# One sequence's attention steps moved five tiles forward in a one-core Macaron block

## The reference

```python
def ffn(x):                                   # 12 experts, 3 for each token
    topw, sel = jax.lax.top_k(x @ Wg, 3)
    cw = sum(softmax(topw) * one_hot(sel, 12))
    h = gelu(einsum('bsd,edh->ebsh', x, Wup) + bup)
    y = einsum('ebsh,ehd->ebsd', h, Wdown) + bdown
    return einsum('bse,ebsd->bsd', cw, y)
def attn(x):
    u = silu(x @ Wg + bg) * (x @ Wi + bi)
    y = Cp * causal_convolution(u, Bp * A ** t) + Dp * u
    y = norm(y) * gamma + beta
    return (silu(y @ Wfg + bfg) * (y @ Wfu + bfu) @ Wfd + bfd) @ Wo + bo
x = x + 0.5 * ffn(layernorm(x))
x = x + attn(layernorm(x))
x = x + 0.5 * ffn(layernorm(x))
```

## Time and profile before

| what | value |
|---|---|
| median of 3 runs | 605.25 us (604.11 to 606.78) |
| the profiled execution | 604.38 us, its span 602.6 us |
| PE busy | 556.8 us (92%) |
| ACT busy | 513.7 us (85%) |
| POOL busy | 404.8 us (67%) |
| DVE busy | 379.4 us (63%) |
| PE's granted clock, mean | 0.972 of full speed |

### The profile page before, as it was taken

How to read it: one execution, slowest core, us unless ns; L and a number is a source line. 1 busy time by engine, 2 the same in 40 slices (tenths; PEclk the granted TensorE clock), 3 DMA queues, 4 the chain that set the end, 5 groups by cost and what they waited for, 6 DMA issues and landing times.

```text
span 602.6 us, 17483 instructions
## 1 busy us (share of the span) xinstructions
PE 556.8 (92%) x4614; PEld 519.1 (86%) x4614; DVE 379.4 (63%) x1787; ACT 513.7 (85%) x1462; POOL 404.8 (67%) x424
## 2 busy tenths in 40 slices
PE   8789889999999999999899889999899999999973
PEld 8689889999999888888799778878899999999941
DVE  7987899791112787988877569988738422232232
ACT  4557998889989899888999799897799999999852
POOL 1076577777767777757677775367777777777771
PEclk8789999999999999999999989998999999999996
DMA  7997242435464343322354342122355433332164
GB/s 199 318 234 226 56 137 85 129 86 135 129 175 117 97 119 92 86 67 69 116 151 125 84 124 77 54 77 68 91 140 139 123 94 87 103 91 67 59 233 139
DMA packets 99127, 72.29 MB, mean 120 GB/s; under 512 B 13519, under 2 KB 91909, under 8 KB 99032
## 3 DMA queue, kind: packets, MB, share of 16 engines
q1 hardware_dynamic: 83032, 43.62, 26.3%
q0 software_dynamic: 13024, 26.11, 15.2%
q10 hardware_dynamic: 2976, 1.44, 0.8%
HBM read 37.08 MB, written 34.75 MB: 119 GB/s over the span
## 4 chain that ended last, share of the span: by engine, by line
PE 42%; POOL 17%; issue 12%; DVE 11%; ACT 9%; DMA 7%; ACTq 1%; POOLq 0%; DVEq 0%; SPq 0%
PE ps L1027 16%; PE ps L1042 15%; POOL YG L831 12%; DMA YG<-ys,SY 4%; POOL yk L841 3%; ACT hT L1215 3%; DMA yk<-Ys,row 2%; POOL xs L812 2%; PE ps L1017 2%; PE ps L997 2%; DVE Ys L2144 1%; DVE st L1284 1%; ACT WT L1098 1%; PE ps L913 1%; PE ps L941 1%
## 5 line engine op out<-in xcount | busy, mean ns | idle before, releaser
L1215 ACT ACTIVATE hT<-ps,BU 128x128 f32<-128x128 f32 x900 | 262.1, 395 | 27.8 <-PE ps L1027 18.0
L1027 PE MATMUL ps<-xT,WT 128*128 128x128 f32 x1800 | 242.0, 278 | 10.0 <-ACT hT L1215 6.9
L1042 PE MATMUL ps<-WD,hT 128*128 x1800 | 239.1, 276 | 0.8 <-DVE Ys L2144 0.8
L1027 PEld LDWEIGHTS ps<-xT,WT 128*128 128x128 f32 x1800 | 221.4, 193 | 20.3 <-issue 18.7
L1042 PEld LDWEIGHTS ps<-WD,hT 128*128 128x128 f32 x1800 | 220.2, 193 | 1.6 <-issue 1.6
L812 POOL DMA_INDIRECT xs<-XN,SX x144 | 142.7, 991 | 67.1 <-issue 58.5
L831 POOL DMA_INDIRECT YG<-ys,SY x132 | 130.7, 990 | 42.4 <-issue 35.7
L1098 ACT ACTIVATE WT<-WU 128x512 f32 x225 | 150.9, 672 | 7.8 <-DVE eW L1761 3.4
L2144 DVE TENSOR_TENSOR Ys<-ps,BD 128x128 f32<-128x128 f32 x225 | 53.7, 285 | 119.6 <-PE ps L1042 112.9
L841 POOL DMA_INDIRECT yk<-Ys,row x71 | 70.8, 997 | 22.1 <-issue 10.7
L799 POOL DMA_INDIRECT xl<-xna,SG x24 | 23.0, 958 | 35.6 <-DMA xna<-XN 27.1
(11 more groups left out here) (403 smaller groups left out, 610.5 us busy)
## 6 DMA issues: line engine op xcount, KB each, us to landing
ys<-Ys SPq DMA_DIRECT2D x41, 256.0 KB, 2.4
xl<-xs SPq DMA_DIRECT2D x94, 64.0 KB
xl<-xs SPq DMA_DIRECT2D x71, 66.0 KB
WU<-in_L_ffn_Wup_dram SPq DMA_DIRECT2D x12, 256.0 KB, 4.7
WD<-in_L_ffn_Wdown_dram SPq DMA_DIRECT2D x12, 256.0 KB, 4.8
YG<-yk SPq DMA_DIRECT2D x4, 768.0 KB, 8.5
xs<-XN,SX POOLq DMA_INDIRECT x144
YG<-ys,SY POOLq DMA_INDIRECT x132
```

What stands on the lines that cost most here:

```text
L1027: x = e.matmul(HB[i % 2][:, c * P:(c + 1) * P], WT[i % NW][:, c, :], xT[m % 2][:, j * P:(j + 1) * P], start=True, stop=True)
L1042: x = e.matmul(YB[u % 2][:, j * D:(j + 1) * D], hT[i % 3][:, c * P:(c + 1) * P], WDf[:, bass.ds(r + c * P, P)], start=(c == 0), stop=(c == ...
L1215: x = e.activation(hT[i % 3][:, c * P:(c + 1) * P], HB[i % 2][:, c * P:(c + 1) * P], ACT.Gelu, bias=BU[:, bass.ds(b + c, 1)])
```

## The change

Column 4 of `CHAIN` (sequence 4) is lowered by five in all 23 rows. The other columns, the tiles and POOL's list stay. SP's and POOL's instructions stand in the same order as before.

```diff
-    ("V", "G0", (8, 13, 19, 27, 54, 58, 65, 72)),
+    ("V", "G0", (8, 13, 19, 27, 49, 58, 65, 72)),
...
-    ("PV", "K", (33, 38, 44, 53, 75, 81, 86, 90)),
+    ("PV", "K", (33, 38, 44, 53, 70, 81, 86, 90)),
```

## The result

| | before | after |
|---|---|---|
| median, us | 605.29 (604.11 to 606.78, 4 runs) | 615.86 (615.0 to 616.8, 4 runs) |
| ratio to before, 95% interval | | 1.0167 [1.0146, 1.0188] |
| the profiled execution, its span, us | 604.38, 602.6 | 615.49, 613.8 |
| PE, ACT, POOL, DVE busy, us | 556.8, 513.7, 404.8, 379.4 | 556.2, 513.9, 404.5, 379.4 |

The changed kernel is slower by 10.6 us, 8.8 to 11.4 by the interval; the forecast was 8.1 us and 613.3, with a range from 605.5 to 617.5. No engine has more to do: busy times agree within 0.6 us. What was added is waiting.

A forecast was written before the change was run, and what follows sets the result against it. POOL's queue of about 170 us without a rest behind K.6 was taken to set the end. The terms 6.3 - 5.4 + 7.2 + 0 = +8.1 us on the median 605.25 gave 613.3 us; range 605.5 to 617.5.

The forecast's parts named there:

- The bound: End of the kernel: it comes when K.6 (tile 146) is ready, plus a fixed POOL queue of about 170 us.
- Tiles 109 to 119: From tile 109, G0.4 and S1.4 on a DVE without rest: new PE waits of 6.3 us.
- Tiles 122 to 130: PE's waits around A1.5, A4.4 and A5.4 and the slow clock behind A1.5 go: -5.4 us.
- K.4: Tiles 128 to 130: PE waits 7.2 us for K.4 behind 12.0 us of DVE work; from 4 to 9.
- Tiles 131 to 150: DVE is lighter, but later PE waits hang on sequences 5 to 7: 0, between -2 and +2 us.
- The sum: At K.6, all terms together: +8.1 us, carried by POOL to the end, 613.3 us on the median; chance 0.62.
- slow clock: Rival: two clock falls of 1.5 us more behind two of the three new waits, 616.3 us; chance 0.12.
- Given back: Rival: behind tile 131 a lighter DVE lets sequences 5 to 7 recover 7 us, 606.3 us; chance 0.15.
- Faster: Rival: DVE has slack, no new wait forms and the 5.4 us go, 599.9 us; chance 0.11.

The follow-up runs named there:

- k6_late: The kernel before with K.6 alone two tiles later (148) on PE and DVE: 611.96 us, ratio to before 1.0090.
- k4_back: The changed kernel with K.4 alone put back to tile 135 on PE and DVE: 611.99 us, ratio to before 1.0118.
- early_only: The kernel before with only G0, G2, S1 and G of sequence 4 five tiles forward: 610.45 us, ratio to before 1.0089.
- g0_behind: The changed kernel with G0.4 alone two tiles later (111): 615.97 us, ratio to before 1.0153.
- c1_late: The kernel before with only C1, C2 and C3 of sequence 4 one tile later (123): 601.62 us, ratio to before 0.9940.
- tail_back: The changed kernel with T, N, N', L and K of sequence 4 put back by five tiles on all engines: 610.26 us, ratio to before 1.0076.
- two_only: The kernel before with all 23 rows of sequence 4 two tiles forward instead of five: 609.80 us, ratio to before 1.0060.
- two_head: The kernel before with only G0 to A5 of sequence 4 two tiles forward: 604.19 us, ratio to before 0.9969.
- two_c1: The kernel before with sequences 4 to 7 two tiles forward and C1 to C3 of sequence 4 one tile later against neighbours: 601.91 us, ratio 0.9942.

## Why the prediction held, point by point

- **The bound.** "K.6 is ready plus a fixed queue of about 170 us": held, and shown by k6_late (a delay of K.6 alone comes out in full at the end) and k4_back (a delay of sequence 4's scatter does not).
- **Tiles 109 to 119.** Forecast 2.1 + 2.1 + 1.5 + 0.6 = 6.3; measured 2.13 + 1.69 + (0.45 + 0.93) + 0.62 = 5.82. The mechanism, moved work in a stretch of DVE without rest, is shown by early_only and g0_behind. S1.4 was to end near 325.0; it ended at 326.46, which is 324.8 without the 1.67 us that this run was behind. The prediction missed that the second wait does not need A1.4: ACT's Gelus stand behind G.4, and take it by themselves (2.79 us in early_only).
- **Tiles 122 to 130.** Forecast -5.4. All of it went: no wait at A1.5 and A5.4 and no low clock there (A4.4 still waits, at its new place; its 0.62 is counted above). c1_late shows the cause, DVE's empty wait for C1.4, by taking that alone away: -3.4 us by the medians against the -3.9 expected. The 1.5 us of low clock in this term were less certain than the waits: early_only kept the wait at A1.5 (1.92 us) and had no low clock behind it.
- **K.4.** Forecast +7.2 by 12.0 us of DVE's work; measured 7.12 by 11.9. k4_back corrects what it means: the wait belongs to the pile, not to K.4, and moving K.4 alone wins 3.9 us (615.9 to 612.0; 2.8 by the traces up to tile 147).
- **Tiles 131 to 150.** This is the term that was mis-sized: forecast 0, from -2 to +2. Measured are 3.86 us of waits against 2.45 before, and 1.7 us of low clock behind K.4 against 1.1 at tile 145 before: about +2.0. The sum took no fall of the clock behind the new waits; the longest did have one. The rival "slow clock" was right in kind and put the price at two falls of 1.5 us; one fall came, and it cost 1.7 us, more than the "at most" 1.5 of the prediction. That the waits of 2.13 and 1.69 us had none is luck as far as these traces tell (last section). The argument against this rival, that part of a slow stretch is covered, is borne out by k4_back (there too).
- **The sum.** 5.8 - 5.4 + 7.1 + 2.0 = 9.5 us by the traces and 10.6 by the medians, against 8.1. The range "from 609 to 616.5 (K.4's wait from 4 to 9 us)" does not follow from that wait alone, which makes 610.1 to 615.1. "Given back" came to 1.7 us and not 7: from tile 135, where both kernels have done nearly the same steps, to tile 147 after comes back from 12.97 us behind to 11.24. Nearly all of that stands at tiles 138 and 140 (0.8 and 0.9 us), where before waits 0.69 us ahead of A7.5 and 0.43 ahead of A4.6 and after does not. "Faster" needed slack on DVE that the trace did not show.

## What to carry to other kernels

A step that is moved forward takes its work along, and on an engine that takes its instructions in order the question is whether the new stretch has a rest of that length: G0.4's 2.1 us of DVE in a stretch without one cost PE 2.1 us, whatever the order in it. A step put at the head of a queue before its input is there holds back all that stands behind it, so look for idle time that ends on another engine with ready work behind it: three steps moved by one tile (c1_late) won 3.4 us where 23 steps moved by five lost 10.6. When a wait is found at one step, test by moving that step alone whether the wait goes or only meets the next one.

## What the runs showed of the hardware

Waits of PE of nearly one length, at the same step, were followed by a fall of the granted clock in some kernels and not in others. L.6 is the step at 410.41 us in the kernel before.

| step | PE's wait, us | a fall behind it | none |
|---|---|---|---|
| tile 113 | 2.06 to 2.13 | k4_back | after, tail_back, early_only |
| A1.5 | 1.92, 1.93 | before, k6_late | early_only |
| L.6 | 1.00, 1.01 | before, k4_back, g0_behind, two_only, two_head | after, tail_back, early_only, c1_late, k6_late, two_c1 |

At tile 113 the one fall stands behind the shortest of the four waits. The windows views of k4_back (tile 113), early_only (A1.5) and before (L.6):

```profile
319.57:322.98 3.41, 3.41 (x20) 3.35 (x20) 2.88 (x16) 3.41 (x12) 2.50 (x4) 0.50 0.17 46
355.23:360.61 5.38, 4.93 (x28) 3.53 (x29) 4.24 (x25) 5.38 (x18) 4.16 (x5) 1.00 0.58 154
412.46:415.88 3.42, 3.42 (x19) 3.42 (x18) 3.04 (x27) 2.94 (x9) 2.50 (x4) 0.50 0.40 117
```

With one trace of each kernel it stays open whether a fall belongs to the kernel or to the single execution.

What a fall costs depends on the next wait. Tiles 113 and 114 took 5.42 us in k4_back and 3.90 in the kernel before, 1.5 us more. But A1.4 then waited only 0.16 us, where it waited 1.69 in after:

```profile
328.98 0.66 PE L887 MATMUL ps<-ident,XN 128*128 128x128 f32 x4 [0.16 <-ACT XN L1121]
```

So tile 118 started 19.64 us behind tile 112 in k4_back and 19.72 in after: DVE set that time, and the fall ahead of it cost nothing.

The waits of 2.79 us in early_only, 2.94 in k4_back, 4.04 in g0_behind and 7.12 in after each had a fall. The Trainium skill's page "TensorE: Matmul & The Clock Gate" (section "Part 1: The HAM clock gate") says that the clock goes down after idleness and comes back after activity. The trace agrees for these four waits; for those in the table the length of a wait by itself did not tell.
